# A transformer-like kernel of eight images: every layer norm cut into quarters of seven tiles and spread over other steps

## What is computed

```
x = x + conv0(ln_c(x))     # all-pairs: xn = v/|v|; y = relu(xn xn^T)^2 (v W)
t = t + moe(ln_t(t))       # softmax gate, top 2 of 16 experts, hidden 128, silu(h1)*h2
x = x + dcn(ln_c(x))       # deformable 3x3 conv: 9 taps at learnt offsets, bilinear from 4 corners
t = t + ffn(ln_t(t))       # the tokens of each image with the 1567 largest router weights
```

## Time and profile before

| | |
|---|---|
| median of 3 runs | 4729.69 us (4725.49 to 4734.18) |
| profiled execution | 4742.12 us, span 4740.3 us |
| mean granted TensorE clock | 0.87 |
| PE / DVE / ACT / POOL busy | 3846.4 / 3248.4 / 2527.1 / 2293.1 us |

### The profile page before, as it was taken

One profiled execution on the slowest core, in us unless ns is written; L12 is line 12 of the kernel. 1 busy time (PEld: TensorE's weight loads), 2 busy tenths in 40 slices (PEclk: granted clock), 3 DMA queues, 4 the chain that ended last, 5 costly groups with the idle time before them and its releaser, 6 DMA issues. The chain is left out here.

```text
span 4740.3 us, 62792 instructions
## 1 busy us (share of the span) xinstructions
PE 3846.4 (81%) x23768; PEld 2126.4 (45%) x23768; DVE 3248.4 (69%) x4592; ACT 2527.1 (53%) x4198; POOL 2293.1 (48%) x2021
## 2 busy tenths in 40 slices
PE   5968996899889989899888988999889989742222
PEld 3533453455544554455544564455545554331112
DVE  5355567777677678767777677867777768745544
ACT  5644764566545665477546665576456655420001
POOL 0000074555455574556455554557455545647770
PEclk9979997999899989999899989999899989865555
DMA  3000121132222231232212222222223212333370
GB/s 97 1 7 0 28 76 52 57 87 62 62 62 58 80 81 52 61 83 65 62 59 62 77 73 60 61 77 77 55 61 84 62 49 75 90 78 91 87 156 21
DMA packets 348667, 306.94 MB, mean 65 GB/s; under 512 B 278336, under 2 KB 282800, under 8 KB 348368
## 3 DMA queue, kind: packets, MB, share of 16 engines
q0 software_dynamic: 96768, 231.34, 16.6%
q1 hardware_dynamic: 251600, 71.62, 7.1%
HBM read 252.58 MB, written 50.24 MB: 64 GB/s over the span
## 5 line engine op out<-in xcount | busy, mean ns | idle before, releaser
L333 POOL DMA_INDIRECT G<-corner_table,index x2016 | 2292.5, 1137 | 2271.1 <-DVE value L379 1007.3
L1109 ACT ACTIVATE work<-PS,descale 128x448 f32<-128x448 f32 x896 | 567.5, 634 | 693.9 <-PE PS L1197 683.9
L1042 ACT ACTIVATE work<-PS 112x784 f32<-112x784 f32 x896 | 727.3, 824 | 339.0 <-PE PS L1197 252.7
L567 DVE TENSOR_TENSOR work<-work 112x784 f32<-112x784 f32 x560 | 542.4, 972 | 424.1 <-PE PS L1197 333.0
L371 DVE TENSOR_TENSOR G<-G,corner_w 112x768 f32<-112x768 f32 x672 | 625.7, 951 | 182.0 <-DMA G<-corner_table,index 181.9
L670 DVE SCALAR_TENSOR_TENSOR work<-PS,descale,work 128x448 f32<-128x448 f32 x896 | 600.3, 680 | 212.2 <-ACT work L1109 208.7
L1197 PE MATMUL PS<-xn_hl,xn_hh 128*112 128x392 f16 x1792 | 634.1, 354 | 96.2 <-ACT work L1042 68.2
L1197 PE MATMUL PS<-work,xj 112*64 112x392 f32 x3584 | 695.1, 501 | 0.0
L1197 PE MATMUL PS<-xn_hl,xn_ll 128*112 128x392 f16 x1792 | 610.6, 341 | 0.0
L1197 PE MATMUL PS<-work,w3s 128*64 128x448 f32 x1792 | 453.4, 584 | 125.1 <-DVE small L666 120.6
L1197 PEld LDWEIGHTS PS<-xn_hl,xn_hh 128*112 128x112 f16 x1792 | 239.9, 134 | 441.3 <-ACT work L1042 203.4
(11 more groups left out here) (231 smaller groups left out, 5122.5 us busy)
## 6 DMA issues: line engine op xcount, KB each, us to landing
G<-corner_table,index POOLq DMA_INDIRECT x2016
corner_table<-xln SPq DMA_DIRECT2D x64, 392.0 KB
corner_table<-G SPq DMA_DIRECT2D x8, 841.0 KB, 10.1
xin<-x SPq DMA_DIRECT2D x8, 784.0 KB, 6.5
x_scratch<-xB SPq DMA_DIRECT2D x7, 784.0 KB, 6.4
yw_scratch<-yw SPq DMA_DIRECT2D x7, 784.0 KB, 6.4
x<-x_scratch SPq DMA_DIRECT2D x4, 784.0 KB, 6.6
split<-yw_scratch SPq DMA_DIRECT2D x4, 784.0 KB, 10.5
```

The source lines that it names most:

```text
L333: GP.indirect_dma_start(G[0:TP, t % 2, tap * 4 * C:(tap + 1) * 4 * C], None, tables[b % 2], bass.IndirectOffsetOnAxis(ap=index[:, col:col ...
L567: V.tensor_tensor(sq[:, u % 4], relu[:, u % 2], relu[:, u % 2], ALU.mult).then_inc(s["sq_dve"], 1)
L1042: A.activation(relu[:, u % 2], PS[u % 2][0:TP, :, 0:IW], ACT.Relu).then_inc(s["relu_done"], 1)
L1109: A.activation(silu[:, e % 2, :], S[e % 2][:, 0:CW], ACT.Silu, scale=descale[:, MOE1:MOE1 + 1]).then_inc(s["silu_done"], 1)
```

## The change

Every norm is cut into four quarters of seven tiles (`quarter(q)`), with a semaphore step for each, so that the next engine can start on a quarter. The quarters are then set into other places:

- Conv norm (n): up to six pieces in a chunk instead of one. DVE's stand behind experts with e % 8 in (0, 2, 6), ACT's with e % 8 in (0, 3, 5). The two splits of a quarter become one instruction of twice the size (the tokens broadcast over high parts), the two casts as well.
- Norm g: the second gap's DVE part (`geo_start`) now holds also the square (on DVE, not ACT), the second sum and the variance; ACT's square root follows the stacks. Scaling and split stand in quarters in steps 0, 1 and 5 of bodies 0 and 1, ACT's casts and table copies likewise.
- Norm f: `ffn_start` (sum, mean, centring in quarters) stands between the halves of the mixer, ahead of the addition into x1; ACT's squares in body 7; the rest in quarters in bodies 8 to 12. The skip is added after the split and not before.
- Norm a, in the first gap: quarters in the same order; one FFN chunk instead of two is computed there, the other after the gate's shift. PE's transposes wait for the quarters that they need (`quarters_of(c)`), as they do for g and f.
- The transposes of g start a pair of steps earlier (body 1, step 3) and the offset matmuls a pair of steps or more (body 3, step 0); those of f start at body 11, step 1 instead of body 10, step 7. Positions and corner weights are split over more steps; the second group's weights are complete in body 8, step 1 instead of body 7, step 5.
- SP's waits count four quarters where they counted one norm.

```diff
-GEO_EVAC = ((1, 7), (2, 1), (2, 3), (2, 5), (2, 7), (3, 1), (3, 3))
-FFN_EVAC = ((10, 7), (11, 1), (11, 3), (11, 5), (11, 7), (12, 1), (12, 3))
+GEO_EVAC = ((1, 3), (1, 5), (1, 7), (2, 1), (2, 3), (2, 5), (2, 7))
+FFN_EVAC = ((11, 1), (11, 3), (11, 5), (11, 7), (12, 1), (12, 3), (12, 5))
+NORM_DVE, NORM_ACT = (0, 2, 6), (0, 3, 5)
...
+        def quarter(q):
+            return slice(q * T // 4, (q + 1) * T // 4)
+        def quarters_of(c):
+            return (CT * (c + 1) - 1) * 4 // T + 1
...
+            def norm_piece(k, n):
+                if n == 4:
+                    ln_mean(2)
+                if n == 17:
+                    norm_invert(k)
+                for q in range(4):
+                    if n == q:
+                        red(st[:, 2, 0, quarter(q)], xin[:, quarter(q), :])
+                    if n == 4 + q:
+                        ln_center("n", xm, xin, 2, q)
+                    if n == 11 + q:
+                        ln_square_sum("n", k, tmp, 2, q)
+                    if n == 17 + q:
+                        norm_first(q)
+                    if n == 21 + q:
+                        norm_second(q)
+                    if n == 27 + q:
+                        norm_split(k, q)
+                if n == 14:
+                    norm_var(k)
...
-            def geo_center(i):
-                dve.drain()
-                ln_sum(xB[i % 2][:, :, :], 0)
+            def geo_start(i):
+                x2 = xB[i % 2]
+                dve.drain()
+                ln_sum(x2[:, :, :], 0)
+                ln_mean(0)
                 if i > 0:
                     dve.wait_ge(s["table_written"], i * 128)
-                ln_center("g", xln, xB[i % 2][:, :, :], 0)
+                V.tensor_tensor(xln[:, :, :], x2[:, :, :], bc(st[:, 0, 1, :], 2, C), ALU.subtract)
+                dve.drain()
+                V.tensor_tensor(tmp[:, :, :], xln[:, :, :], xln[:, :, :], ALU.mult)
+                dve.drain()
+                red(st[:, 0, 2, :], tmp[:, :, :])
+                ln_var("g", 0, LNC_EPS)
...
+            def ffn_start(f):
+                x3 = xB[f % 2]
+                dve.drain()
+                ln_sum(x3[:, :, :], 1)
+                ln_mean(1)
+                if f > 0:
+                    dve.wait_ge(s["yw_stored"], f * 16)
+                for q in range(4):
+                    ln_center("f", yw, x3, 1, q)
...
+                    if k >= 2 and half == 0:
+                        ffn_start(k - 2)
                     for m in range(2):
                         dve.wait_ge(s["y_done"], k * 4 + half * 2 + m + 1)
...
-                    if k + 1 < B and e == 14:
-                        norm_piece(k + 1, c)
+                    for m in range(3):
+                        if k + 1 < B and e % 8 == NORM_DVE[m]:
+                            norm_piece(k + 1, 6 * c + 3 * (e // 8) + m)
...
                     ffn_up(k - 2, 0)
-                    ffn_up(k - 2, 1)
                     ffn_down(k - 2, 0)
-                    ffn_down(k - 2, 1)
...
-                    ffn_rest(k - 2, 2)
+                    ffn_rest(k - 2, 1)
```

More of the change, by code:

```diff
@@ L777, in _ @@
                 image(k)
-            for j in range(BPH + 1):
+            for j in range(BPH + 2):
                 for u in range(SPB):
@@ L785, in _ @@
                             weigh(B - 2, late_tile(j) + 1, piece)
-            for j in range(8, 11):
+            ffn_start(B - 2)
+            for j in range(8, 13):
                 for u in range(SPB):
@@ L1137, in image @@
                     sample_evac(k - 1, BPH - 1, 2)
-                square("a", k, tmp, xm)
+                for q in range(4):
+                    square("a", k, tmp, xm, q)
                 ln_std("a", k, 0)
@@ L1148, in image @@
                 if k >= 2:
-                    for c in range(2, NCH):
+                    for c in range(1, NCH):
                         gelu_chunk(k - 2, c)
@@ L1159, in image @@
                     stacks(k + 1, 0, 3 * NCH)
-            square("n", 0, tmp, xm)
-            norm_std(0)
-            norm_cast(0, 0)
-            norm_cast(0, 1)
+                ln_std("g", k, 0)
+            for n in range(6 * NCH):
+                norm_piece(0, n)
             stacks(0, 0, 3 * NCH)
@@ L1183, in _ @@
                     sample_evac(B - 1, t, n)
-            square("f", B - 1, tmp, yw)
+            for q in range(4):
+                square("f", B - 1, tmp, yw, q)
             ln_std("f", B - 1, 1)
-            cast_h("f", B - 1, 1)
+            for q in range(4):
+                cast_h("f", B - 1, 1, q)
             for c in range(NCH):
```

343 lines of the change are left out of this document (189 added, 154 removed).

## The result

The changed kernel takes 4534.72 us (median of 4 runs, 4532.07 to 4540.7) against 4727.62 us before (4 runs, 4725.49 to 4734.18): a ratio of 0.9589, 95% interval 0.9577 to 0.9600, so 193 us or 4.1% less. The forecast was 4555 us with a range of 4512 to 4635. The profiled execution took 4532.74 us.

A forecast was written before the change was run, and what follows sets the result against it. PE was taken to bound the long stages, interrupted by the norms' 2 us operations on VectorE and ScalarE. Gains of 113 + 45.5 + 8 + 8.3 = 175 us gave a median of 4555 us, range 4512 to 4635.

The forecast's parts named there:

- Chunks 1 to 6: Expert chunks: spreading the conv norm's pieces gains 15.2 us an image, 106 us on seven images; about 190 us afterwards.
- The granted clock: Chunks 1 to 6: the clock falling after longer waits makes PE 11.0 us busier; 0.98 or more expected after the change.
- Rival 2: Chunks: PE's waits shorten but the clock still falls once in each chunk; 77 us less gain, 4632 us; chance 0.12.
- rival 3: Gaps: clock stays up there too, first gap gains 3 us on six images, table loads hide; 4517 us; chance 0.12.
- Mixer: Mixer: fewer PE waits for relu; 7 us on each of images 2 to 7, 3.5 in image 1, together 45.5 us.
- Between the halves: Between mixer halves: FFN norm's sum and centrings, about 4.6 us, hide in VectorE's 5.68 us wait; cost 0.
- Second gap: Second gap: moved square and second sum, 4.3 us, hide in VectorE's 8.07 us idle time; cost 0, wait near 3 left.
- First gap: First gap: images 2 to 7 cancel to 0 (bounds 3 us won, 2 lost an image); images 0 and 1 gain 8.
- Tail: At the end, FFN norm chains: 4.7 us gained for image 7 and 2 for image 6, together 6.7 us.
- Rival 1: VectorE pieces: their fixed cost decides, 0.46 us per quartered operation; 61 us of the gain lost, 4616 us; chance 0.12.
- Rival 4: Chunks: VectorE falls behind at experts 0, 2 and 6, each piece delaying PE fully; slower, 4815 us; chance 0.04.
- Rival 5: Whole kernel: PE was idle for other reasons than these operations, nothing measurable changes, 4730 us; chance 0.02.

## Why the forecast held, step by step

**Chunks 1 to 6: right.** 106 us forecast, 101.2 measured; about 190 us for the six chunks forecast and 191.0 measured in image 3, with the clock at 0.99. That VectorE's operation at the chunk's end is what stops PE, and that its place counts, is shown by the kernel with the same pieces in a row (202.8 us). The conv norm alone, 4610.22 us, gave 114.6 us, of which 113 were forecast with chunk 0. What remains over image 7 is 6.4 us, forecast 5.7. By the additions of the chunks, in image 3 chunk 2 takes 33.9 us where an undisturbed one takes 30.9, chunk 4 33.6 us with a wait of 1.76 us at its end, and the other four are within 0.4 us of image 7's. So 3.0 of the 6.4 us are chunk 2's, which holds the table loads and the inverse together. I had named the loads for 3 us; 0.63 us of PE's waiting stands right behind them, and their share of the 2.30 us is open.

**The granted clock: right in direction, and half of the gain in the chunks.** Before, chunks 1 to 6 of image 3 ran at 0.94 and PE was busy 183.72 us; after, 0.99 and 175.87; the stretch at the lower clock fell from 22.9 to 3.4 us. Rival 2 (the clock falls once a chunk all the same) is out. In the first gap the clock did not rise (0.75 in its window, before 0.80 in one 4.8 us longer), so rival 3 is out too.

**Mixer: right in mechanism, half in size.** This is the term that was mis-sized: 45.5 forecast, 88.1 measured. I left 3.7 of 10.7 us of relu waits; 1.7 remained. That is 2 us an image. The larger part is the step "So 7 us on each of images 2 to 7", which counted waits for the relu only. From PE's first product to its first with W of the second half, image 3's mixer took 219.1 us and takes 205.3, a gain of 13.8 us. All waits of PE there over 0.15 us fell from 14.3 to 5.3 us, which is 9.0, all of it the relu's. The stretch at the lower clock fell from 13.0 to 7.3 us, and PE does in 5.7 us at half clock what takes 2.85 at full, so about 2.9 more. The last 1.9 us lie in what the profile counts as PE's busy time (its shorter gaps fell by only 0.1 us), and what they are is open. The clock was the term I had priced in the chunks and forgotten in the mixer, though its row said 0.97.

**Between the halves: right.** VectorE's idle time was forecast at about 1 us from 5.68, and is 0.95; PE's wait for the addition is 0.7 us in image 3. **Second gap: small miss.** The prediction calls the square and second sum that move there the conv norm's; they are norm g's, and the price is the same. The 4.3 us moved to VectorE were to be free under 8.07 us of idle time. The idle time behind them is 1.29 us, where I said 3. ScalarE's square root and copy come 0.7 us later in each of seven images, 4.9 us in the table. The conv norm alone, which does not touch this gap, shows 60.3 us there. PE's first product of the next mixer starts 9.03 us after the start of the last addition into xB, and 9.2 before. So PE is not held up. What the cuts put on this gap, and another 0.2 us an image, they take from the first half after it: counted from PE's first products the mixer gained 82 us and not 88, and the gap lost nothing.

**First gap: near in sum, not in its parts.** The stage gained 10.9 us where I had put 15, 8 for norm a and 7 for chunk 0. Images 0 and 1 gained 8.2 and 4.3 us, forecast 5.5 and 4.5 with their chunk 0; images 2 to 7 lost 1.6 us together, where chunk 0 was to give 5. In them PE's wait moved to gelu as the row of 4.21 us had warned: 6.14 us now. "The two cancel: 0" was a fair call between its bounds, a little on the losing side, by about 8 us over the kernel if the run with the chunk put back is taken at its median. **Start: right**, 1.6 us. **Tail:** 6.7 us forecast. The table says 12.5, but the tail took 619.7 us with its old code in the conv norm's kernel, and 613.1, 616.5, 617.1 and 618.3 in the four profiles of the first chip with the new: 1 to 7 us.

**The sum: nearer than its terms.** The profiled executions differ by 209 us and the medians by 193, where 175 was forecast for both. The mixer's term was too low by 43 us (37 from PE's first products) and the others together too high by some 8; another 16 us of the stage sums are the slow profiled execution before. That the median came within 20 us of the forecast is in part luck.

**The rivals.** Rival 1 rested on 0.46 us per quartered operation. It is 0.20, and the kernel that pays it without spreading was not slower than the one that does not. Rival 4 needed a delay of 0.6 us per piece; PE's waits for hid over chunks 1 to 6 are 6.6 us where they were 7.4, so there was none on balance. Rival 5 is excluded by the interval. All of this holds for the first chip. On the second the changed kernel gained 43 us, outside of what any of the rivals was made for: I had taken the chip itself for given.

## What to carry to other kernels

When a stage is paced by one engine and another engine's whole-image operation stands ahead of something it waits for, look for a stretch of the same work without it (here image 7) and cost the difference, clock included, in every stage. The cut itself does not pay, it is what lets the work be spread: cutting at the same place won next to nothing in the chunks, spreading won 90 us. Do not take work out of a gap in which the main engine waits for a third one, and confirm a gain of a few per cent on a second chip.

## What the runs showed of the hardware that I had not expected

The same program took 4534.72 us on one chip and 5022.83 on another, 10.8% more, and the kernel before 4727.62 and 5066 to 5074, 7% more. The image without gathers took the same time on both, and DMA packets and busy times of ScalarE and VectorE were the same; the difference is in stalls of ScalarE and VectorE of up to 13.7 us, and of PE of up to 6.0 us behind them. Those that the profile calls remote end with a semaphore of PE that rises microseconds behind the recorded end of PE's instruction (669 of 4883 rises by more than 1 us, against 2 of 5210 on the first chip). With norm f's operations back at their old places PE's late rises all but vanish from the mixer's second halves (4 and 10 against 111), with norm g's they halve in the first (55 against 121). Their cause is open. The recorded 0.62 us of an operation of 448 elements on VectorE overlap the next one: it starts 0.54 us later, four in a row take 2.23 us, and a whole one of 1792 elements 2.03.
